# Two self-attention layers on one core: the rows of negated maxima by matmul and copy, or by two DMAs through device memory

## The chip, the cores and the metric

One core of a Trainium2 chip runs the whole program. The metric is device time in microseconds (us), the median of several executions; the profile comes from one further execution.

## What is computed

The input x has 4 images of 256 channels and 64 x 64 = 4096 positions. Layer 0 is self-attention over all positions, layer 1 is self-attention whose keys and values are max-pooled 2 x 2 to 1024 positions. Cut to what matters:

```
# layer 0, per image, xf = x as (256, 4096)
q = Wq @ xf + bq ; k = Wk @ xf + bk ; v = Wv @ xf + bv      # 32, 32, 256 rows
attn = softmax(q.T @ k, over the axis of q)
x = gamma * (v @ attn) + xf
# layer 1, on that x
theta = theta_w @ x + theta_b                               # 32 x 4096
phi, g = maxpool2(phi_w @ x + phi_b), maxpool2(g_w @ x + g_b)  # 32 x 1024, 128 x 1024
out = g @ softmax(theta.T @ phi, over the 1024).T
y = gamma * (out_w @ out + out_b) + x
```

All in float32. Softmax subtracts the row's maximum, so the maximum of each row of scores must be known before its exponentials.

## The kernel before

**Tiles, chunks and steps.** The 4096 columns that are softmaxed are cut into 8 chunks of 512 (`NCH`). A chunk of layer 0 takes 32 steps, one for each tile of 128 keys, a chunk of layer 1 takes 8. The order of images is layer 0, then layer 1, then the next image. In each step TensorE makes the scores of the tile that is `AHEAD` = 3 steps on (`scores`, L798), ScalarE takes two exponentials of them (L505 in float32, L508 rounded), GpSimd makes the rounding remainder `prob_l` (L446), VectorE adds the exponentials to a running sum `acc` (L637), and TensorE multiplies values by probabilities, three matmuls (L821, L824, L825) per half of the value rows: six in layer 0, three in layer 1 (`attend`).

**The maxima.** The scores are computed a first time, transposed, only for their maxima. A job `ST` is one matmul of 128 columns' queries against 512 keys into a PSUM bank (L861) and a VectorE `TENSOR_REDUCE` of it (L675, `maximum`). A chunk of layer 0 needs 32 of them, a chunk of layer 1 needs 8. They run one chunk ahead, between the other matmuls. After the last one VectorE reduces to four columns of negated maxima (L681), rounds them (L683) and takes the remainder (L684): pairs (high, low), one value per partition. They must become two rows of 512 columns under the queries, since the matmul of the scores adds them by two rows of ones in the keys. That is job `M`: TensorE transposes by four matmuls against the identity (L866), and VectorE copies the rows from PSUM to `queries` (L694). `scores` of a chunk's first tile waits for that copy (L793).

**Banks.** There are eight PSUM banks. X0 (`aux0`) and X1 (`aux1`) serve the jobs, Y is the second output bank where layer 1 doesn't use it. A job's matmul waits until the bank's last user has freed it: VectorE for `ST`, `D2`, `V0L`, ScalarE for `Z`.

**Other jobs.** `D1` and `D2` sum the exponentials and spread the reciprocals over partitions (L870, L698, L874); `Z` is the output projection of layer 1 (L878), copied out by ScalarE (L584) and added by GpSimd as `ZA` (L471); `N` is the residual add of layer 0 on GpSimd (L465); `X` and `XL` round the inputs (L546, L455); `K0`, `V0`, `K1`, `G1`, `T1` and their `..L` parts are projections (L835, L895) whose remainders VectorE makes (L653, L654).

**The order.** `make_plan` writes the order out by hand: `put(g, place, job)` hangs a job on step g; place 1 is before the first half of `attend`, place 2 between the halves, place 3 after. Each engine walks the same list and does its part of each job, in order. `before[...]` holds long lists at the start of layer 1. SyncE (queue SP) has its own loop: store a finished chunk (L415), wait for the store, load the chunk that is four on (L406).

Of the kernel before, what the change touches and what calls it, by code (L numbers as in the profile page):

```python
# [25 lines left out]
P = 128  # L26
DK = C // 8
# [65 lines left out]
def make_plan():  # L93
# [36 lines left out]
    for b in range(B):  # L130
        more = b + 1 < B
        for n in range(NCH):
            g = tile_no(0, b, n)
            prev = chunk_before(0, b, n)
            if prev is not None:
                put(g, 1, on(Job("D2", *prev, 0), X1))
                if prev[0] == 0:
                    c = prev[2]
                    put(g + 1, 1, Job("N", *prev, 0))
                    put(g + 3, 1, Job("N", *prev, 1))  # L140
                    put(g + 5, 1, Job("X", 1, b, c, 0))
                    put(g + 6, 1, Job("XL", 1, b, c, 0))
                    put(g + 8, 1, Job("XL", 1, b, c, 1))
                    put(g + 10, 1, on(Job("K1", 1, b, c, 0), X1))
                    put(g + 11, 1, Job("K1K", 1, b, c, 0), Job("K1Q", 1, b, c, 0))
                    put(g + 12, 1, Job("K1M", 1, b, c, 0), Job("K1L", 1, b, c, 0))
                    put(g + 13, 3, on(Job("G1", 1, b, c, 0), X1))
                    put(g + 15, 1, on(Job("T1", 1, b, c, 0), X1))
                    put(g + 16, 1, Job("T1L", 1, b, c, 0))
                else:  # L150
                    for k in range(CT):
                        put(g + 3 + 2 * k, 1, on(Job("Z", *prev, k), X1))
                        put(g + 4 + 2 * k, 1, Job("ZA", *prev, k))
            put(g + 22, 1, Job("XB", 0, b, n, 0))
            if n + 1 < NCH:
                steps = [(i, X0) for i in range(27)] + [(i, X1) for i in range(20, 25)]
                steps.sort()
                for i, (t, at) in enumerate(steps):
                    put(g + t, 1 if at == X1 else 3, maxima(0, b, n + 1, i // SUBS, i % SUBS, at))
                put(g + 28, 1, on(Job("M", 0, b, n + 1, 0), X1))  # L160
            else:
                for i in range(SUBS * (NCH - 1)):
                    put(g + i, 3, maxima(1, b, i // SUBS, 0, i % SUBS, X0))
# [28 lines left out]
        for n in range(NCH):  # L192
            g = tile_no(1, b, n)
            if n:
                prev = (1, b, n - 1)
                put(g, 1, on(Job("D2", *prev, 0), X0))
                for k in range(CT):
                    put(g + 2 + 2 * k, 3, on(Job("Z", *prev, k), X0))
                    put(g + 3 + 2 * k, 3, Job("ZA", *prev, k))
                if n + 1 < NCH:  # L200
                    put(g + 1, 1, on(Job("M", 1, b, n + 1, 0), Y))
# [3 lines left out]
            else:  # L205
                for s in range(SUBS):
                    put(g + s, 3, maxima(1, b, 1, 1, s, X0))
                put(g + 4, 3, on(Job("M", 1, b, 1, 0), X0))
            put(g + KT[1] - 1, 2, on(Job("D1", 1, b, n, 0), X0))
            if n + 2 < NCH:  # L210
                for s in range(SUBS):
                    put(g + 4 + s, 3, maxima(1, b, n + 2, 1, s, Y))
            if more:
# [3 lines left out]
                else:  # L217
# [747 lines left out]
```

## Time and profile before

| | us |
|---|---|
| three runs, median (lowest to highest) | 2790.31 (2786.36 to 2790.55) |
| the profiled execution, its own time | 2785.08 |
| its span, first to last instruction | 2783.3 |

Mean granted clock of TensorE: 0.984 of full speed. One chunk of layer 0 takes 64.3 us, one of layer 1 from 12.8 to some 22 us. The span has 39336 instructions. Times in the profile are from the span's start; L12 is line 12 of the kernel; "PE" is TensorE, "PEld" its weight loads, "DVE" VectorE, "ACT" ScalarE, "POOL" GpSimd, "SP" SyncE. Matmuls are pipelined: two matmuls of 512 columns start 0.23 us apart although each lasts 0.4 us, so a time on TensorE is read from start to start.

### The profile page before, as it was taken

The page shows a single profiled execution, that of the slowest core. Times are in us where ns is not written, and L with a number is a line of the kernel's source. Part 1 is how long each engine was busy: PE and PEld are TensorE (multiplying, and loading weights), DVE is VectorE, ACT ScalarE, POOL GpSimd, SP SyncE. Part 2 cuts the span into 40 slices and gives each one's busy share as a digit, 9 for nine tenths or more (in the row PEclk, how much of TensorE's full clock was granted, in tenths as well). Part 3 has the DMA queues.
Part 4 walks back from the last instruction along what each step waited for, and adds up shares of the span by engine and source line. Part 5 has one row for each costly group of instructions (what it writes and reads, how often), then busy time and mean ns, then how long its engine had stood idle before and what let it go on. Part 6 is the DMA issues. An engine that isn't in the chain of part 4 may idle for free.

```text
span 2783.3 us, 39336 instructions
## 1 busy us (share of the span) xinstructions
PE 2693.6 (97%) x12260; PEld 2159.1 (78%) x12260; DVE 2004.2 (72%) x3303; ACT 1745.2 (63%) x3171; POOL 1956.3 (70%) x1544
## 2 busy tenths in 40 slices
PE   7999999999999999998999999999899999999988
PEld 5788888877688888887778888888767888888866
DVE  7677777767767777776776777777676777777665
ACT  5566666666756666666765566666676666666657
POOL 3677777767767767776786767777577677777768
PEclk9999999999999999999999999999999999999989
DMA  2000000012110000001211000000121000000011
GB/s 86 1 16 24 16 24 16 16 39 69 61 38 16 24 16 16 16 16 38 69 65 35 24 16 16 16 16 16 46 76 61 16 16 16 16 16 16 16 46 61
DMA packets 43194, 85.03 MB, mean 31 GB/s; under 512 B 2672, under 2 KB 2800, under 8 KB 42992
## 3 DMA queue, kind: packets, MB, share of 16 engines
q1 hardware_dynamic: 35360, 68.17, 7.2%
q10 hardware_dynamic: 7632, 14.36, 1.8%
q8 instruction: 104, 1.70, 0.3%
q14 instruction: 98, 0.80, 0.1%
HBM read 48.96 MB, written 33.55 MB: 30 GB/s over the span
## 4 chain that ended last, share of the span: by engine, by line
PE 87%; DVE 4%; issue 3%; ACT 3%; POOL 2%; DMA 0%; POOLq 0%; ACTq 0%; DVEq 0%
PE o_ps L821 18%; PE o_ps L824 18%; PE o_ps L825 18%; PE s_ps L798 10%; PE aux L861 9%; PE aux L835 2%; PE aux L874 2%; PE aux L870 2%; DVE mx L675 2%; PE aux L895 1%; POOL prob_l L446 1%; PE aux L839 1%; PE aux L878 1%; ACT queries L530 1%; PE o_ps L861 1%
## 5 line engine op out<-in xcount | busy, mean ns | idle before, releaser
L446 POOL TENSOR_TENSOR prob_l<-prob,prob_h 128x512 fp32r<-128x512 f32 x1280 | 1640.6, 1289 | 717.4 <-ACT prob_h L508 706.0
L505 ACT ACTIVATE prob<-s_ps 128x512 f32<-128x512 f32 x1280 | 767.3, 599 | 819.8 <-PE s_ps L798 817.2
L675 DVE TENSOR_REDUCE mx<-aux 128x1 f32<-128x512 f32 x1103 | 760.7, 690 | 424.0 <-PE aux L861 419.0
L821 PE MATMUL o_ps<-prob_h,vh 128*128 128x512 f32 x2304 | 926.8, 402 | 0.5 <-ACT prob_h L508 0.4
L824 PE MATMUL o_ps<-prob_l,vh 128*128 128x512 f32 x2304 | 904.6, 393 | 1.4 <-POOL prob_l L446 1.3
L825 PE MATMUL o_ps<-prob_h,vl 128*128 128x512 f32 x2304 | 903.1, 392 | 0.0
L637 DVE TENSOR_TENSOR acc<-prob,acc 128x512 f32<-128x512 f32 x1216 | 836.4, 688 | 26.8 <-ACT prob L505 11.4
L508 ACT ACTIVATE prob_h<-s_ps 128x512 fp32r<-128x512 f32 x1280 | 762.1, 595 | 0.0
L798 PE MATMUL s_ps<-queries,keys 128*128 128x512 f32 x1280 | 524.3, 411 | 17.9 <-DVE queries L694 10.8
L824 PEld LDWEIGHTS o_ps<-prob_l,vh 128*128 128x128 f32 x2304 | 436.7, 190 | 97.7 <-POOL prob_l L446 5.0
L825 PEld LDWEIGHTS o_ps<-prob_h,vl 128*128 128x128 f32 x2304 | 434.6, 189 | 99.7
L821 PEld LDWEIGHTS o_ps<-prob_h,vh 128*128 128x128 f32 x2304 | 438.5, 190 | 94.4 <-ACT prob_h L508 3.4
L861 PE MATMUL aux<-keys,queries 96*128 96x512 f32 x1103 | 442.8, 401 | 14.2 <-ACT zc L584 5.1
L798 PEld LDWEIGHTS s_ps<-queries,keys 128*128 128x128 f32 x1280 | 245.7, 192 | 86.7 <-DVE queries L694 23.5
L861 PEld LDWEIGHTS aux<-keys,queries 96*128 96x128 f32 x1103 | 208.1, 189 | 77.0 <-DVE mx L675 15.9
L675 DVE TENSOR_REDUCE mx<-o_ps 128x1 f32<-128x512 f32 x159 | 109.2, 687 | 62.9 <-PE o_ps L861 62.3
L634 DVE COPY acc<-prob 128x512 f32<-128x512 f32 x64 | 44.3, 692 | 103.8 <-ACT psums L527 101.8
L455 POOL TENSOR_TENSOR xl<-xa,xh 128x512 fp32r<-128x512 f32 x72 | 92.1, 1285 | 24.9 <-ACT xh L546 24.9
L455 POOL TENSOR_TENSOR xl<-xp,xh 128x512 fp32r<-128x512 f32 x56 | 71.6, 1286 | 54.0 <-ACT xh L546 54.0
L465 POOL TENSOR_TENSOR xa<-osb,xa 128x512 f32<-128x512 f32 x64 | 83.2, 1303 | 20.9 <-DVE osb L707 20.9
L861 PE MATMUL o_ps<-keys,queries 96*128 96x512 f32 x159 | 83.6, 526 | 5.2 <-DVE mx L675 4.0
L471 POOL TENSOR_TENSOR xa<-zc,xa 128x512 f32<-128x512 f32 x64 | 83.1, 1300 | 6.0 <-ACT zc L584 4.8
(122 smaller groups left out, 1947.9 us busy)
## 6 DMA issues: line engine op xcount, KB each, us to landing
xa<-x SPq DMA_DIRECT2D x32, 512.0 KB, 3.7
spill<-xa SPq DMA_DIRECT2D x32, 512.0 KB, 2.7
xa<-spill SPq DMA_DIRECT2D x32, 512.0 KB, 3.7
y<-xa SPq DMA_DIRECT2D x32, 512.0 KB, 2.7
xp<-x ACTq DMA_DIRECT2D x26, 512.0 KB, 3.7
xp<-x SPq DMA_DIRECT2D x2, 512.0 KB, 9.1
prob<-w_in ACTq DMA_DIRECT2D x1, 576.0 KB, 5.3
wo<-w_out ACTq DMA_DIRECT2D x1, 128.0 KB, 6.1
```

The costliest lines, as they stand in the source:

```text
L446: nc.gpsimd.tensor_tensor(out=prob_l[:, i, :], in0=prob[:, i, :], in1=prob_h[:, i, :].bitcast(f32), op=ALU.subtract).then_inc(pl_ready, 1)
L455: nc.gpsimd.tensor_tensor(out=xl[r % 2][:, k, :], in0=src[:, k, :], in1=xh[r % 2][:, k, :].bitcast(f32), op=ALU.subtract).then_inc(xl_read ...
L465: nc.gpsimd.tensor_tensor(out=xa[slot][:, k, :], in0=osb[:, k, :], in1=xa[slot][:, k, :], op=ALU.add).then_inc(x1_ready, 1)
L505: nc.scalar.activation(prob[:, i, :], s_ps[s][:, :], ACT.Exp).then_inc(p_ready, 1)
L508: nc.scalar.activation(prob_h[:, i, :], s_ps[s][:, :], ACT.Exp).then_inc(ph_ready, 1)
L637: nc.vector.tensor_tensor(out=acc[:, :], in0=prob[:, i, :], in1=acc[:, :], op=ALU.add).then_inc(acc_done, 1)
L675: ins = nc.vector.tensor_reduce(out=dst, in_=bank[:, :], axis=AX.X, op=ALU.max)
L798: mm(s_ps[h % SRING][:, :], keys[l][:, t * P:(t + 1) * P], queries[:, q_slot(l, b, n), :], start=True, stop=True).then_inc(s_full, 1)
L821: mm(o_ps[ct][:, :], value(vh, l, t, ct), prob_h[:, i, :], start=t == 0, stop=False)
L824: mm(o_ps[ct][:, :], value(vh, l, t, ct), prob_l[:, i, :], start=False, stop=False)
L825: last = mm(o_ps[ct][:, :], value(vl, l, t, ct), prob_h[:, i, :], start=False, stop=t == KT[l] - 1)
L861: last = mm(dst[:, :], queries[0:R3, q_slot(l, b, c), sub * P:(sub + 1) * P], keys[l][0:R3, chunk(kc)], start=True, stop=True)
```

## The change

1. `M` leaves the banks, except for the very first chunk and the first chunk of layer 1 of each image (5 of 64). For the other 59, VectorE writes the pairs to a small tile `nm_pair`, SyncE stores it to device memory as two rows of 512 (`nm_rows`), waits for that store, and loads the two rows into `queries`. `scores` of the chunk's first tile waits for the second DMA (`nm_in`).
2. In layer 0 the 32 `ST` of a chunk end at step 23 and no longer at step 26; nine of them and no longer five are on X1, at place 1 of steps 1 to 4 and 19 to 23. `M` stands at step 25 in place of 28.
3. In layer 1 `M` stands at a chunk's step 0 in place of 1 (chunk 0: step 5, place 1, in place of step 4, place 3), and the last four `ST` of the next image's first chunk move from steps 0 and 1 of chunk 7 to steps 4 to 7 of chunk 6.
4. SyncE walks the same list as the other engines, so that its stores, loads and `M` stand in one order; the load behind a store of layer 1 is two steps later.
5. Score matmuls use 98 rows (96 and the pair) where they used 128.

The diff also has a second pair of names, `r_rows` and `scaled`, for `D2` by the same way; in this plan every `D2` is still in a bank, so nothing uses them.

```diff
             if n + 1 < NCH:
-                steps = [(i, X0) for i in range(27)] + [(i, X1) for i in range(20, 25)]
-                steps.sort()
-                for i, (t, at) in enumerate(steps):
-                    put(g + t, 1 if at == X1 else 3, maxima(0, b, n + 1, i // SUBS, i % SUBS, at))
-                put(g + 28, 1, on(Job("M", 0, b, n + 1, 0), X1))
+                steps = sorted(([(t, 3, X0) for t in range(23)]
+                         + [(t, 1, X1) for t in (1, 2, 3, 4, 19, 20, 21, 22, 23)]), key=lambda e: e[:2])
...
+                put(g + 25, 1, Job("M", 0, b, n + 1, 0))
...
                 if n + 1 < NCH:
-                    put(g + 1, 1, on(Job("M", 1, b, n + 1, 0), Y))
+                    put(g, 1, Job("M", 1, b, n + 1, 0))
...
-                put(g + 4, 3, on(Job("M", 1, b, 1, 0), X0))
+                put(g + 5, 1, Job("M", 1, b, 1, 0))
...
-                        put(g + s // 2, 3, maxima(0, b + 1, 0, n, s, (X1, Y)[s % 2]))
-                    put(g + 4, 1, on(Job("M", 0, b + 1, 0, 0), Y))
+                        put(g + 4 + s, 3, maxima(0, b + 1, 0, NCH - 1, s, Y))
+                if n == NCH - 1:
+                    put(g, 1, Job("M", 0, b + 1, 0, 0))
...
+                elif name == "M" and job in ROW_OF:
+                    i = ROW_OF[job]
+                    wait_free(sp, LAST_MAX[l, b, c])
+                    sp.dma_start(nm_rows[row].rearrange("h (s p) -> p (h s)", p=P),
+                                 nm_pair[:, :, :].bitcast(f32).rearrange("p h s -> p (h s)")).then_inc(nm_out, 16)
+                    sp.wait_ge(nm_out, 16 * (i + 1))
+                    wait(sp, nm_in, 16 * i)
+                    sp.dma_start(queries[NM, q_slot(l, b, c), :].bitcast(f32), nm_rows[row]).then_inc(nm_in, 16)
...
+                if rows in BANK:
+                    hi, lo = nm_wide[:, :, R3], nm_wide[:, :, R3 + 1]
+                else:
+                    hi, lo = nm_pair[:, 0, :], nm_pair[:, 1, :]
+                    wait(dve, nm_out, 16 * ROW_OF[rows])
+                chain(nc.vector.tensor_copy(hi, nm))
+                nc.vector.tensor_tensor(out=lo, in0=nm, in1=hi.bitcast(f32), op=ALU.subtract).then_inc(free[BANK[job]], 1)
...
                 if t == 0:
-                    wait_free(pe, Job("M", l, b, n, 0))
+                    rows = Job("M", l, b, n, 0)
+                    if rows in BANK:
+                        wait_free(pe, rows)
+                    else:
+                        pe.wait_ge(nm_in, 16 * (ROW_OF[rows] + 1))
...
-                mm(s_ps[h % SRING][:, :], keys[l][:, t * P:(t + 1) * P], queries[:, q_slot(l, b, n), :],
+                mm(s_ps[h % SRING][:, :], keys[l][0:R3 + 2, t * P:(t + 1) * P], queries[0:R3 + 2, q_slot(l, b, n), :],
                    start=True, stop=True).then_inc(s_full, 1)
```

**TensorE at steps 27 and 28 of a chunk of layer 0**, before (`s_ps` banks take the scores, `o_ps` the output, `aux1` is X1):

```order
L825 MATMUL o_ps1<-prob_h,vl0 128x512
L798 MATMUL s_ps1<-queries,keys0 128x512 [waits ph_ready]
L866 MATMUL aux1<-ident_r,nm_wide 128x128 [waits free0,free1]
L866 MATMUL aux1<-ident_r,nm_wide 128x128 x3
L821 MATMUL o_ps0<-prob_h,vh0 128x512 [waits ph_ready,free3]
```

In the change the four L866 rows are gone there, and on SP stand these (`free1` is the last maximum on X1):

```order
L455 DMA nm_rows<-nm_pair 128x8x1 [waits free1]
L459 DMA queries<-nm_rows 2x512 [waits nm_in,nm_out]
L433 DMA spill<-xa 128x2x512 [waits x1_ready]
L424 DMA xa<-spill 128x2x512 [waits xl_ready,xa_out0]
```

The rows' way moved from TensorE and VectorE to SP, ahead of the next chunk's store.

**TensorE at step 3 of chunk 0 of layer 0 of the second image**, before:

```order
L798 MATMUL s_ps2<-queries,keys0 128x512 [waits ph_ready]
L878 MATMUL aux1<-osb,wo 128x512 [waits free1]
L821 MATMUL o_ps0<-prob_h,vh0 128x512 [waits ph_ready,free3]
L824 MATMUL o_ps0<-prob_l,vh0 128x512 [waits pl_ready]
```

and now:

```order
L865 MATMUL s_ps2<-queries,keys0 128x512 [waits ph_ready]
L945 MATMUL aux1<-osb,wo 128x512 [waits free1]
L928 MATMUL aux1<-keys0,queries 128x512 [waits free5,free1]
L888 MATMUL o_ps0<-prob_h,vh0 128x512 [waits ph_ready,free3]
L891 MATMUL o_ps0<-prob_l,vh0 128x512 [waits pl_ready]
```

A matmul for maxima now follows `Z` (L945) into the same bank X1, ahead of the step's value matmuls. At step 19 of the same chunk one follows `V0` of step 17 in the same way, where X1 is freed by `V0L`, itself at step 19.

## Rows read from the trace of the kernel before

**Rows 1.** The page: busy time by engine, and the chain that ended last.

```profile
PE 2693.6 (97%) x12260; PEld 2159.1 (78%) x12260; DVE 2004.2 (72%) x3303; ACT 1745.2 (63%) x3171; POOL 1956.3 (70%) x1544
...
PE 87%; DVE 4%; issue 3%; ACT 3%; POOL 2%; DMA 0%; POOLq 0%; ACTq 0%; DVEq 0%
```

**Rows 2.** Windows: stretch, its length, busy us by engine, PEclk, DMA share, GB/s.

```profile
266.00:330.30 64.30, 64.30 (x290) 52.44 (x290) 47.24 (x78) 39.43 (x74) 45.98 (x36) 1.00 0.05 17
2695.10:2707.90 12.80, 12.71 (x62) 9.39 (x61) 9.69 (x19) 10.65 (x21) 12.55 (x11) 1.00 0.23 80
624.30:627.20 2.90, 2.90 (x14) 2.86 (x13) 1.14 (x2) 0.15 (x2) 2.73 (x3) 0.50 0.00 0
```

**Rows 3.** Timeline, TensorE, steps 28 and 29 of a layer-0 chunk: start, us, instruction.

```profile
321.79 0.56 PE L866 MATMUL aux<-ident_r,nm_wide 128*128 128x128 f32 x4
322.19 0.45 PE L821 MATMUL o_ps<-prob_h,vh 128*128 128x512 f32 x1
322.47 0.40 PE L824 MATMUL o_ps<-prob_l,vh 128*128 128x512 f32 x1
...
323.98 0.40 PE L821 MATMUL o_ps<-prob_h,vh 128*128 128x512 f32 x1
...
325.58 0.39 PE L821 MATMUL o_ps<-prob_h,vh 128*128 128x512 f32 x1
```

**Rows 4.** Waits: who waited for whom, us in total, times, longest.

```profile
PEld s_ps L798 <- DVE queries L694: 23.5, 39, 2.7
...
PE s_ps L798 <- DVE queries L694: 10.8, 8, 2.4
```

**Rows 5.** Timeline, chunk 0 of layer 1: the pairs ready, and the scores behind them.

```profile
619.01 0.17 DVE L684 TENSOR_TENSOR nm_wide<-aux,nm_wide 128x4 fp32r<-128x4 f32 x1
...
622.69 0.50 PE L798 MATMUL s_ps<-queries,keys 128*128 128x512 f32 x1 [2.36 <-DVE queries L694]
...
2676.16 0.17 DVE L684 TENSOR_TENSOR nm_wide<-aux,nm_wide 128x4 fp32r<-128x4 f32 x1
...
2677.89 0.50 PE L798 MATMUL s_ps<-queries,keys 128*128 128x512 f32 x1 [0.51 <-DVE queries L694]
```

**Rows 6.** Timeline, later chunks of layer 1: pairs ready, and scores at step 5.

```profile
727.00 0.17 DVE L684 TENSOR_TENSOR nm_wide<-o_ps,nm_wide 128x4 fp32r<-128x4 f32 x1
...
733.73 0.80 PE L798 MATMUL s_ps<-queries,keys 128*128 128x512 f32 x1
...
2709.61 0.17 DVE L684 TENSOR_TENSOR nm_wide<-o_ps,nm_wide 128x4 fp32r<-128x4 f32 x1
...
2716.51 0.40 PE L798 MATMUL s_ps<-queries,keys 128*128 128x512 f32 x1
```

**Rows 7.** Timeline, chunk 0 of layer 0, second image, steps 3 and 19.

```profile
761.70 1.02 PE L878 MATMUL aux<-osb,wo 128*128 128x512 f32 x2
...
762.87 0.79 ACT L584 ACTIVATE zc<-aux,cb,cols 128x512 f32<-128x512 f32 x1
...
798.38 0.40 PE L798 MATMUL s_ps<-queries,keys 128*128 128x512 f32 x1
...
799.79 0.68 DVE L653 TENSOR_TENSOR vl<-aux,vh 128x512 fp32r<-128x512 f32 x1
```

**Rows 8.** Timeline, steps 0 and 1 of a layer-0 chunk, then two reductions in layer 1.

```profile
330.85 1.40 DVE L707 SCALAR_TENSOR_TENSOR osb<-osb,cols,aux 128x512 f32<-128x512 f32 x2
...
332.19 0.40 PE L798 MATMUL s_ps<-queries,keys 128*128 128x512 f32 x1
...
704.49 1.28 DVE L675 TENSOR_REDUCE mx<-aux 128x1 f32<-128x512 f32 x2
```

**Rows 9.** DMA: a queue's packets and share, then issues, KB each, median us to landing.

```profile
q1 hardware_dynamic: 35360, 68.17, 7.2%
...
spill<-xa SPq DMA_DIRECT2D x32, 512.0 KB, 2.7
xa<-spill SPq DMA_DIRECT2D x32, 512.0 KB, 3.7
```

More of the change, by code:

```diff
@@ L272 @@
         LAST_READ.append(Job("G1", 1, _job.b, _job.c, 0) if _job.l else Job("V0", 0, _job.b, _job.c, 1))
+    if _job.name in ("M", "D2") and _job not in BANK:
+        ROW_OF[_job] = sum(j.name == _job.name for j in ROW_OF)
     if _job.name in ("K0", "V0", "K1Q", "K1K", "T1"):
@@ L429, in _, with entry @@
                     load_a(nxt // NCH % 2, nxt // (2 * NCH), nxt % NCH)
+            def entry(job):
+                name, l, b, c, k = job
+                row = chunk_no(l, b, c)
+                if name in ("N", "ZA") and k == CT - 1:
+                    store_a(l, b, c)
+                elif name == "XL" and l == 1 and k == CT - 1:
+                    reload(0, b, c)
+                elif name == "M" and job in ROW_OF:
[6 more added lines that the diff above has]
+                    sp.dma_start(queries[NM, q_slot(l, b, c), :].bitcast(f32), nm_rows[row]).then_inc(nm_in, 16)
+                elif name == "D1" and Job("D2", l, b, c, 0) in ROW_OF:
+                    i = ROW_OF[Job("D2", l, b, c, 0)]
+                    wait_free(sp, job)
+                    sp.dma_start(r_rows[row].rearrange("(s p) -> p s", p=P), rsum[:, :]).then_inc(r_out, 16)
+                    sp.wait_ge(r_out, 16 * (i + 1))
+                    wait(sp, scaled, i)
+                    sp.dma_start(rb[:, :], r_rows[row:row + 1, :].broadcast_to([P, CH])).then_inc(r_in, 16)
+            for p in range(ASLOTS + PSLOTS):
+                load_p(p)
+            late = {}
+            with nc.allow_non_contiguous_dma(reason="rows of one value per partition"):
+                for g in range(TILES):
+                    for job in late.get(g, ()):
+                        reload(*job[1:4])
+                    for job in BEFORE.get(g, ()):
+                        entry(job)
+                    for e in DURING.get(g, ()):
+                        entry(e.job)
+                        if e.job.name == "ZA" and e.job.k == CT - 1:
+                            late.setdefault(g + 2, []).append(e.job)
+                for job in END:
+                    entry(job)
             for slot in range(ASLOTS):
@@ L699, in entry @@
                 elif name == "D2":
-                    wait_full(dve, job)
+                    if job in BANK:
+                        wait_full(dve, job)
+                        recip, done = bank, free[BANK[job]]
+                    else:
+                        dve.wait_ge(r_in, 16 * (ROW_OF[job] + 1))
+                        recip, done = bank, scaled
                     dve.wait_ge(o_act, chunk_no(l, b, c) + 1)
@@ L865, in entry @@
                     for s in range(SUBS):
[L866 removed]
+                        last = mm(dst[0:R3 + 2, s * P:(s + 1) * P], nm_wide[:, s, :], ident_r[:, :], start=True, stop=True)
                 elif name == "D1":
```

91 lines of the change are left out of this document (49 added, 42 removed).

## The prediction

> **What bounds the kernel now.** I read the page first: TensorE is busy 97% of the span and holds 87% of the chain that ended last [rows 1]. The windows say where this is literally so. A chunk of layer 0 is 64.30 us with TensorE busy for all of them, VectorE for 47.24, GpSimd for 45.98 [rows 2]: in layer 0 a matmul that goes is time that goes, and a wait of TensorE that comes is time that comes. In layer 1 it is narrower: a chunk of the last image takes 12.80 us with GpSimd busy for 12.55 [rows 2], so TensorE can give back 0.25 us there before GpSimd takes over. The remaining question is how job `M` sits in this, and that is read from the timeline and the waits.
>
> **What the removed job costs.** At step 28 the four transposes start at 321.79, and the second value matmul at 322.47 [rows 3]. Five single steps apart from it, value matmuls are 1.60/7 = 0.229 us apart (323.98 to 325.58 is one step of seven matmuls [rows 3]), so without `M` that second matmul would stand at 321.79 + 0.23: `M` costs 0.45 us of TensorE. From 322.47 to 323.98 are six matmuls, which is 1.37 us at that pace; it took 1.51. The 0.14 us are the scores waiting for VectorE's copy of the rows, part of the 23.5 us in 39 times that weight loads of the scores wait for L694 [rows 4]. So a chunk of layer 0 gives back 0.45 + 0.14 = 0.59 us, and 28 of them **16.5 us**. In layer 1, chunks 1 to 6 carry one `M` each: for three images 18 x 0.45 = **8.1 us**, for the last one GpSimd caps it, 6 x 0.25 = **1.5 us**. `M` of the next image's first chunk (3) stands in chunk 7, where steps have four matmuls and GpSimd is the longer: nothing. VectorE's copies (59) are at nothing too, since VectorE has 17 us to spare per layer-0 chunk [rows 2]; its part in the critical stretches of layer 1 is inside the 0.45 us. Score matmuls with 98 rows in place of 128: matmuls of 96 rows already run at the same pace beside them, so nothing. Sum of gains: 26.1 us.
>
> **What the two DMAs take.** No row shows such a DMA, 1024 runs of 4 bytes out and two rows of 2 KB back, so I bound it. A 512 KB store lands 2.7 us after issue; queue 1 spent 7.2% of 16 x 2783.3 us on 35360 packets, 0.091 us each [rows 9]. The store's 256 packets on 16 DMA engines are then 16 x 0.091 = 1.5 us, and 1.2 us are fixed. The load, 3.7 us, has 2.2 us fixed on the same reckoning [rows 9]. First hop: 64 packets per engine. At no cost for their few bytes it takes 1.2 us, at a full packet's 0.091 us each 7.0. Second hop: one packet on each of a few engines, 1.2 to 3.7 us. Together 2.4 to 10.7 us. I take **4.5 us**, nearer the lower end: 4 KB in total are less than a hundredth of the store's bytes, and the row it is nearest to in bytes is the fixed part of store and load, 1.2 + 2.2 = 3.4 us, to which I add 1.1 for the 64 small packets. The Trainium skill, DMA: Bandwidth & Descriptors, section Anatomy of one DMA, gives about 2 us fixed to any DMA of GpSimd's queue, whatever its size; two such in place of the 3.4 us would make the sum 2.4 us higher (0.6 us at four waits). The trace's store, on SyncE's queue, is below it with 1.2.
>
> **Where the scores would wait.** The window is from the pairs being ready to the scores of the next chunk. Layer 1, the narrowest of the first image: 727.17 to 733.73, less the 0.45 us of `M` that was in it, 6.1 us; last image 2709.78 to 2716.51, 6.3 us [rows 6]. Layer 0: the last maximum is now at step 23 and the scores at step 29, a step with one extra matmul (1.83 us) and five of 1.60, 9.8 us, less some 2.9 us (an estimate: two reductions and a sum at 0.64 each, and the matmul and the small operations around them) until the pairs are ready: 6.9 us. 4.5 us fit in all of them. They don't fit in chunk 0 of layer 1, where the maxima of chunk 1 end at step 3 and the scores stand at step 5: pairs ready at 619.18, scores at 622.69 after a wait of 2.36 already [rows 5]. With 4.5 us they go to 623.7, 1.0 us later, three times; in the last image 2676.33 + 4.5 = 2680.8 against 2677.89, 2.9 us later [rows 5]. Sum **5.9 us**. Behind these waiting scores on TensorE stands everything else of it, and ScalarE, GpSimd and VectorE run dry after it. On SP nothing urgent is queued behind an `M`; but `M` is queued behind a load of 512 KB in the chunks of layer 1, which can add up to its 2.2 us to the first hop, inside the window at 4.5.
>
> **What the packing costs.** Per chunk of layer 0 the same 32 matmuls and reductions remain. Steps 1 to 4 now have two. At step 1 the one on X1 needs `D2` off the bank: VectorE ends at 330.85 + 1.40 = 332.25, TensorE would come at 332.19 + 0.23 = 332.42 [rows 8]: no wait, by 0.15 us. In a step with two, TensorE needs 9 x 0.23 = 2.07 us and VectorE three operations of 0.64 (two reductions in a row take 1.28 [rows 8]), 1.92 us: it keeps up. So nothing in the ordinary chunk. In chunk 0 of the next image (three times) X1 has other users. At step 3 the matmul follows `Z` at once: it could start at 761.70 + 0.46 = 762.16 and must wait for ScalarE's copy, done at 763.66 [rows 7]: 1.5 us. At step 19 it could start at 798.38 + 0.23 and must wait for `V0L`, done at 800.47 [rows 7]: 1.85 us. 3 x 3.35 = **10.1 us**. Moving four `ST` from chunk 7 to chunk 6 of layer 1 adds 4 x 0.23 = 0.9 us there and takes as much off chunk 7, in which TensorE is left with little and GpSimd, 12.55 us in a chunk [rows 2], is the longer: I count even.
>
> **The clock.** After the wait of 2.36 us the granted clock was 0.50 from 624.30 to 627.20 [rows 2], the 1.2 GHz level instead of 2.4: half of 2.9 us, 1.5 us lost. How short a wait may be and still be followed by one I can't read from this. Of the six new waits and the longer one in the last image I let half be followed by one: 3.5 x 1.5 = **5.3 us**.
>
> **Sum:** -26.1 + 5.9 + 10.1 + 5.3 = -4.8 us. The profiled execution took 2785.1 us, so 2780.3 for its like; the median shown is 2790.3, so **2785.5 us**, 0.17% less. A measurement of this kernel tells about 0.2% (5.6 us) from no change.
>
> **Rivals.** *1. As summed* (0.42): between about -10 and +3 us, as the clock and the second digit of the hops fall; mostly within 0.2%, 0.12 of it beyond on the fast side, 0.02 on the slow. *2. The new waits on X1 are cheaper* (0.24): if ScalarE and VectorE stand earlier than in the rows, or what TensorE loses comes back since its neighbours catch up, 10.1 + 5.3 us shrink to some 3, and the sum is -17: 2773 us. For it: ScalarE idles before L584's step; against: in layer 0 TensorE has no slack in which it could catch up [rows 2]. *3. Long hops* (0.20), the other side: it decides where the two DMAs exceed the windows, from 6.1 us on. At 7 us, chunk 1 costs 10 us more than summed, layer 1 about 9 for some 12 narrow chunks at 0.7 to 0.9, layer 0 3 us: +17, 2807 us; every further microsecond costs some 50 us. Upper bounds of both hops give 10.7 us, so the rows don't exclude it. For a mechanism: each 4-byte run is its own packet, and the packets may cost far more than their bytes. The Trainium skill, same page, Specifications, says a transfer under 512 B becomes a read-modify-write, which is this rival; no packet like it is in this trace. *4. The packed steps bind* (0.07): the 0.15 us at step 1 is missing and each chunk loses 0.4 us more, 11 us: +6, 2797 us. *5. The rows' way was hidden anyway* (0.07), so that the change doesn't give what it says: another engine holds each place, layer 0's 16.5 us are half, +3 us: 2794 us.
>
> **How the numbers follow.** Faster: 0.12 + 0.24 = 0.36. Within 0.2%: 0.28 + 0.04 of rival 4 + 0.06 of rival 5 = 0.38. Slower: 0.02 + 0.20 + 0.03 + 0.01 = 0.26. The likeliest is case 1, alone 2779 to 2793. The range reaches to rival 2 and to rival 3 at 7 us, 2772 to 2807, and leaves out longer hops.
>
> **What would show it.** Right: the value matmuls of layer 0 run through at 0.23 us with no gap where L866 was; L866 has 20 matmuls; the DMA part lists `nm_rows<-nm_pair` and `queries<-nm_rows` at some 2.7 and 1.8 us, 59 each; the waits list scores for a DMA four times, 3.4 us for the first three and about 3.5 for the last; L928 waits three times each for L584's successor and for `V0L`. Wrong: scores waiting for a DMA 28 times in layer 0 or throughout layer 1 (hops over 6 us), waits of VectorE's reductions in steps 1 to 4, or L928 without those six waits.

## The result, and the profile after

| | us |
|---|---|
| before, four runs, median (lowest to highest) | 2788.8 (2786.4 to 2790.6) |
| the change, four runs | 3203.5 (3200.1 to 3207.3) |
| ratio, 95% interval | 1.149 (1.147 to 1.151) |
| the profiled execution of the change, its span | 3198.3 |

The change makes the kernel 415 us slower. The page of its profile: busy time by engine, then the chain that ended last, by engine and by line (cf. [rows 1]):

```profile
PE 2792.8 (87%) x12024; PEld 2216.5 (69%) x12024; DVE 1961.2 (61%) x3244; ACT 1748.2 (55%) x3171; POOL 1955.7 (61%) x1544
...
PE 66%; DMA 24%; DVE 6%; issue 2%; ACT 1%; POOL 0%; POOLq 0%; ACTq 0%; DVEq 0%
```

A quarter of the chain is now DMA, where it was 0%. The waits for it (engine, what for: us in total, times, longest; cf. [rows 4]):

```profile
PEld s_ps L865 <- DMA queries<-nm_rows: 357.5, 59, 13.2
...
PE s_ps L865 <- DMA queries<-nm_rows: 328.8, 59, 12.8
...
PE aux L928 <- DVE vl L706: 5.2, 3, 1.7
```

All 59 rows that come by DMA are waited for, 5.6 us each on average, where I expected four waits. One of them in the chain of waits (start, us, what), at the end of the first chunk of layer 0:

```profile
124.31 0.17 DVE nm_pair L743
124.48 0.02 issue
124.50 9.38 DMA nm_rows<-nm_pair
133.87 0.02 issue
133.89 3.24 DMA queries<-nm_rows
137.13 0.04 issue
137.17 0.80 PE s_ps L865
```

The pairs are ready at 124.48, the scores start 12.7 us later after a wait of 5.34. Without it they would have stood at 131.8: the window is 7.3 us (I had worked out 6.9), and the hops are what does not fit. The store alone takes 9.38. The view of the DMA engines for 124.4 to 134.0, in 40 slices of 0.24 us, shows where:

```profile
DMA  0000576000000000000000000000000000000000
...
DMA packets 1040, 0.00 MB, mean 0 GB/s; under 512 B 1040, under 2 KB 1040, under 8 KB 1040
```

All packets lie in three slices, some 0.9 to 1.6 us after the issue. Then the engines do nothing that a row shows, for nearly 8 us, until the store counts as done. Over the whole run the DMA part says the same (KB each, median us to landing; cf. [rows 9]):

```profile
nm_rows<-nm_pair SPq DMA_DIRECT2D x59, 4.0 KB, 10.6
```

The clock adds to it. Windows at the same wait (columns as in [rows 2]):

```profile
133.00:137.20 4.20, 0.03 (x1) 0.03 (x1) 0.00 (x0) 0.00 (x0) 0.00 (x0) 0.64 0.01 1
137.20:141.00 3.80, 3.80 (x9) 3.04 (x10) 0.00 (x0) 1.09 (x3) 1.27 (x1) 0.50 0.00 0
141.00:145.00 4.00, 4.00 (x22) 3.42 (x22) 1.57 (x3) 2.65 (x5) 2.43 (x2) 1.00 0.00 0
```

TensorE idles, and for 3.8 us after it the granted clock is 0.50, the 1.2 GHz level: half of 3.8 us, 1.9 us, is lost behind the wait. The mean granted clock fell from 0.984 to 0.925. At half speed in the slow stretches that is 2 x 0.075 x 3198 = 480 us of them, 391 us more than before. By the clock's records in the trace 155 us of them lie inside the 59 waits, where they cost nothing. The other 236 us cost half of their length, 118 us or 2.0 us for each wait.

A chunk of layer 0, from one reciprocal to the next (287.57 to 359.49), takes 71.9 us where it took 64.3 [rows 2].

### The profile page after: what moved, and what is told of

It reads as the page before. It is cut to its first block, busy times and chain, and to the rows that moved or that the text cites. A ratio compares the mean times of both kernels' runs of the same rounds, so it can differ in the third digit from the quotient of the medians.

```text
span 3198.3 us, 38986 instructions
## 1 busy us (share of the span) xinstructions
PE 2792.8 (87%) x12024; PEld 2216.5 (69%) x12024; DVE 1961.2 (61%) x3244; ACT 1748.2 (55%) x3171; POOL 1955.7 (61%) x1544
## 4 chain that ended last, share of the span: by engine, by line
PE 66%; DMA 24%; DVE 6%; issue 2%; ACT 1%; POOL 0%; POOLq 0%; ACTq 0%; DVEq 0%
DMA nm_rows<-nm_pair 19%; PE o_ps L888 14%; PE o_ps L891 14%; PE o_ps L892 14%; PE s_ps L865 8%; PE aux L928 8%; DMA queries<-nm_rows 4%; DVE mx L728 2%; PE aux L902 2%; DVE acc L690 1%; PE aux L941 1%; PE aux L937 1%; PE aux L906 1%; PE aux L962 1%; PE o_ps L928 1%
## 5 line engine op out<-in xcount | busy, mean ns | idle before, releaser
L888 PE MATMUL o_ps<-prob_h,vh 128*128 128x512 f32 x2304 | 956.8, 415 | 0.5 <-ACT prob_h L561 0.4
L891 PE MATMUL o_ps<-prob_l,vh 128*128 128x512 f32 x2304 | 939.5, 408 | 1.3 <-POOL prob_l L499 1.3
L892 PE MATMUL o_ps<-prob_h,vl 128*128 128x512 f32 x2304 | 929.0, 403 | 0.0
L865 PE MATMUL s_ps<-queries,keys 98*128 98x512 f32 x1280 | 554.6, 434 | 338.7 <-DMA queries<-nm_rows 328.8
L865 PEld LDWEIGHTS s_ps<-queries,keys 98*128 98x128 f32 x1280 | 260.0, 204 | 425.1 <-DMA queries<-nm_rows 357.5
L891 PEld LDWEIGHTS o_ps<-prob_l,vh 128*128 128x128 f32 x2304 | 456.6, 198 | 108.0 <-POOL prob_l L499 3.1
L888 PEld LDWEIGHTS o_ps<-prob_h,vh 128*128 128x128 f32 x2304 | 459.1, 199 | 100.5 <-issue 2.7
L892 PEld LDWEIGHTS o_ps<-prob_h,vl 128*128 128x128 f32 x2304 | 453.2, 197 | 108.8
L928 PE MATMUL aux<-keys,queries 96*128 96x512 f32 x1097 | 449.7, 410 | 15.5 <-DVE vl L706 5.2
L508 POOL TENSOR_TENSOR xl<-xp,xh 128x512 fp32r<-128x512 f32 x56 | 71.5, 1285 | 71.7 <-ACT xh L599 69.1
L928 PE MATMUL o_ps<-keys,queries 96*128 96x512 f32 x165 | 93.2, 565 | 7.5 <-DVE mx L728 6.3
## 6 DMA issues: line engine op xcount, KB each, us to landing
nm_rows<-nm_pair SPq DMA_DIRECT2D x59, 4.0 KB, 10.6
```

The costliest lines, as they stand in the source:

```text
L508: nc.gpsimd.tensor_tensor(out=xl[r % 2][:, k, :], in0=src[:, k, :], in1=xh[r % 2][:, k, :].bitcast(f32), op=ALU.subtract).then_inc(xl_read ...
L865: mm(s_ps[h % SRING][:, :], keys[l][0:R3 + 2, t * P:(t + 1) * P], queries[0:R3 + 2, q_slot(l, b, n), :], start=True, stop=True).then_inc(s ...
L888: mm(o_ps[ct][:, :], value(vh, l, t, ct), prob_h[:, i, :], start=t == 0, stop=False)
L891: mm(o_ps[ct][:, :], value(vh, l, t, ct), prob_l[:, i, :], start=False, stop=False)
L892: last = mm(o_ps[ct][:, :], value(vl, l, t, ct), prob_h[:, i, :], start=False, stop=t == KT[l] - 1)
L928: last = mm(dst[:, :], queries[0:R3, q_slot(l, b, c), sub * P:(sub + 1) * P], keys[l][0:R3, chunk(kc)], start=True, stop=True)
```

## The experiments

A run of bytes, in "runs of 4 B", is a stretch of neighbouring bytes in what the DMA writes. "By matmul" is job `M` as before the change; "packed" is point 2 of the change, "unpacked" the steps before it. Medians against the kernel before, timed beside them (2788.3 to 2789.6):

| kernel | rows of maxima by | else | us | ratio (95%) |
|---|---|---|---|---|
| the change | two hops, runs of 4 B | packed, 98 rows | 3203.5 | 1.149 (1.147 to 1.151) |
| E1 | matmul | packed, 98 rows | 2802.7 | 1.004 (1.003 to 1.006) |
| E2 | hops in layer 0 alone | packed, 98 rows | 2989.7 | 1.072 (1.070 to 1.073) |
| E3 | two hops, 4 B | unpacked, 98 rows | 3287.0 | 1.178 (1.176 to 1.180) |
| E4 | two hops, 16 B | packed, 98 rows | 2812.3 | 1.008 (1.006 to 1.009) |
| E5 | one hop, 16 B | packed, 98 rows | 2802.1 | 1.004 (1.003 to 1.005) |
| E6 | one hop, 16 B | E5 without clashes | 2792.6 | 1.001 (1.000 to 1.002) |
| E7 | matmul, every fourth column | packed, 98 rows | 2827.2 | 1.014 (1.012 to 1.015) |
| E8 | VectorE | unpacked, 98 rows | 2866.4 | 1.028 (1.026 to 1.029) |
| E9 | two hops, 128 B | E6's packing, 98 rows | 2782.2 | 0.997 (0.996 to 0.999) |
| E10 | matmul | unpacked, 98 rows | 2799.3 | 1.004 (1.002 to 1.005) |
| E11 | matmul | unpacked, 128 rows | 2787.5 | 0.999 (0.998 to 1.000) |
| E12 | two hops, 128 B | E6's packing, 128 rows | 2765.6 | 0.992 (0.990 to 0.994) |
| **E13** | E12, chunk 1 of layer 1 by matmul | 128 rows | **2756.4** | **0.989 (0.987 to 0.990)** |
| E14, E15, E16 | the kernel before | 98, 127, 112 rows | 2804.3, 2801.2, 2805.5 | 1.006, 1.005, 1.006 (each +-0.002) |

### Where the 415 us are: E1, E2, E3

E1 takes the rows' DMAs out of the change and leaves the rest.

```diff
-                put(g + 25, 1, Job("M", 0, b, n + 1, 0))
+                put(g + 28, 1, on(Job("M", 0, b, n + 1, 0), X1))
```

(and the three other `M` of layer 1 and the next image likewise, as before the change; E2 does it for those three alone, so 28 rows of layer 0 are left with hops.)

> The change with its packing, SyncE's order and 98 rows, but all rows of maxima made by TensorE and VectorE as before (step 28 in layer 0). Theory (all of the loss is the hops): within 2790 to 2805 us, likeliest 2797, the six waits on X1 in chunk 0 of images 1 to 3 and nothing else. Rival (the packed steps bind, or SyncE's order delays transfers): a good part of the 415 us stays, 2850 us or more.

> The change with the two hops in the 28 ordinary chunks of layer 0 only; the 31 others made by matmul and copy. Theory (each row pays its own wait of 5.3 us and some 1.6 us of halved clock, less 0.59 us gained): 28 x 6.3 = 176 us over the kernel with all rows by matmul, about 2970 us (2950 to 2995). Rival (the waits in layer 0 feed on those of layer 1, for instance by the clock): under 2930 us, or the loss nearly whole, over 3050.

E1 took 2802.7, E2 2989.7. So the parts of the change add up: 14 us without any hop, 187 us for the 28 rows of layer 0 (6.7 each), 214 us for the other 31 (6.9 each). Per row, on average over the change: a wait of 5.6 us, some 2.0 of clock behind it, less what `M` gave. Nearly all of the loss is the hops.

E3 keeps the hops and spreads layer 0's maxima over steps 0 to 26 again (27 on X0, five on X1, the lines that the diff removed).

> The change's hops in both layers, but layer 0's maxima spread over steps 0 to 26 as before. Theory (the wait is the hops' 12.7 us less the window between the pairs and the scores): the window shrinks by about 6 us in 28 chunks, 170 us more than the change: about 3370 us (3310 to 3410). Rival (the packing buys nothing, since the transfers are held by something later): within 30 us of 3204.

It took 3287.0, 84 us more than the change, under my range. A chunk of layer 0 went from 71.7 to 76.6 us, so the packing buys 4.9 us of window there and not 6; the chunks of layer 1, summed over four images, took 37 us less than in the change, which I can't explain (the store's median was 9.7 us there, not 10.6). What it shows: given such hops, packing was worth its place.

### What a store of 4-byte runs costs: DMAs alone

Both kernels leave all of the computation out: SyncE issues a DMA, waits for it, issues the next, six of each kind. The 4-byte store is the change's own, and the others differ as the expectation says.

```diff
+                for i in range(REPS):
+                    step(sp.dma_start(d_rows[i].rearrange("h (s p) -> p (h s)", p=P),
+                                      pair[:, :, :].rearrange("p h s -> p (h s)")))
...
+                for i in range(REPS):
+                    step(sp.dma_start(d_apart[i][:, :, 0], pair[:, :, :].rearrange("p h s -> p (h s)")))
```

> Nothing of the layers is computed: SyncE alone issues small DMAs one after the other, each waited for before the next, six of each kind, then copies x to y; its total time means nothing here. Issue to landing of the first hop's store (1024 runs of 4 B into device memory) was 10.6 us in the changed kernel, the load 3.2 us to the scores. Theory A (the number of single 4 B writes to device memory sets it): 1024 runs about 10 us, 512 runs about 6, 256 runs about 4, 256 runs of 16 B about 4, 128 runs of 32 B about 3, 1024 runs of 4 B that lie 64 B apart as slow as those side by side, about 10. Theory B (writes that fall on the same memory line wait for each other): the 1024 runs 64 B apart take under 5 us, those side by side 10. Theory C (load by the kernel's own transfers and engines): all of them take 2 to 3 us here. The load of 2 rows of 2 KB: 2 us in all. The single hop from SBUF to SBUF, 128 runs of 16 B into one row: 2 to 2.5 us by A and B.

The timeline of SyncE's queue (start of the first of six, us to the end of the last issue): one DMA takes a sixth of the time from one group's start to the next group's.

```profile
1.48 48.74 SPq L338 DMA_DIRECT2D rows4b<-pair  x6
60.37 43.25 SPq L341 DMA_DIRECT2D half4b<-pair  x6
113.65 38.70 SPq L343 DMA_DIRECT2D quarter4b<-pair  x6
159.70 7.36 SPq L345 DMA_DIRECT2D pairs32b<-pair  x6
168.14 18.13 SPq L347 DMA_DIRECT2D apart4b<-pair  x6
189.00 6.27 SPq L349 DMA_DIRECT2D two2kb<-flat  x6
196.25 6.95 SPq L351 DMA_DIRECT2D queries<-rows4b  x6
204.43 32.59 SPq L353 DMA_DIRECT2D gathered<-pairs32b  x6
241.91 9.39 SPq L356 DMA_DIRECT2D runs16b<-pair  x6
252.49 9.99 SPq L358 DMA_DIRECT2D onehop<-pair  x6
263.88 17.02 SPq L360 DMA_DIRECT2D onehop<-wide  x6
283.67 0.48 SPq L362 DMA_DIRECT2D onehop<-pair  x1
```

1024 runs of 4 B: (60.37 - 1.48) / 6 = 9.8 us, with nothing else running, so theory C falls. 512 of them 8.9, 256 of them 7.7: the number of runs is not it either, and theory A falls. The same 1024 runs 64 B apart, a partition's eight behind each other: 3.5 us. 128 runs of 32 B 1.4, 256 runs of 16 B 1.8, two rows of 2 KB 1.2, the load of two rows 1.4. A load that gathers 1024 runs of 4 B takes 6.2, so turning the order round on the way back would be no remedy. One hop from SBUF to SBUF takes 1.9 in 128 runs of 16 B and 3.3 in 512 runs of 4 B, where 512 such runs took 8.9 into device memory, so 4 B runs are not so dear where they end in SBUF.

The second kernel varies the distance alone, with neighbouring runs from neighbouring partitions.

> Small DMAs alone again, none of the layers computed: a store of 1024 runs of 4 B from 128 partitions into device memory, the same every time but for the distance of the runs there: 4, 8, 16, 32, 64 B (16, 8, 4, 2 and 1 writes to a line of 64 B, an assumed size). In the first look they took 9.8 us at 4 B and 3.5 us at 64 B. Theory (writes into one line wait for each other, about 0.4 us each): 9.8, 6.7, 5.0, 4.2 and 3.5 us. Rival (a line of 32 B or less, or the span of addresses matters): 3.5 us from 32 B on alike, or 9.8 us at 8 B too. The last kind, eight runs of 4 B of one partition side by side: by the theory 8 writes to 32 B, 16 to a line, about 9.8 us; if only writes from different partitions disturb each other, 4 us or less.

```profile
0.93 48.00 SPq L328 DMA_DIRECT2D every4b<-pair  x6
59.47 21.84 SPq L331 DMA_DIRECT2D every8b<-pair  x6
85.67 14.83 SPq L334 DMA_DIRECT2D every16b<-pair  x6
103.32 14.25 SPq L337 DMA_DIRECT2D every32b<-pair  x6
120.02 12.66 SPq L340 DMA_DIRECT2D every64b<-pair  x6
134.70 36.91 SPq L343 DMA_DIRECT2D own32b<-wide  x6
179.71 0.42 SPq L346 DMA_DIRECT2D big<-x  x1
```

By distance: 9.8 us at 4 B, 4.4 at 8, 2.9 at 16, 2.8 at 32, 2.4 at 64 (3.5 in the first kernel, whose 64 B runs lay in another order). It is steepest at the close end, not 0.4 us per write as my theory had it, and it flattens from 16 B on. Eight runs of one partition side by side, with the next partition's eight behind them, take 7.5, so it isn't writes of different partitions alone. What is shown: neighbouring 4 B writes to device memory delay each other's completion, by 7 us in this shape. The size of the line on which they meet isn't: a fixed 64 B line fits the last steps badly.

The Trainium skill, DMA: Bandwidth & Descriptors, Anatomy of one DMA, says of GpSimd's path that most of a DMA's fixed cost is the memory's receipt for the last byte, without which the semaphore can't rise. The nearly 8 idle us after the last packet look like it, on SyncE's queue. The whole fixed cost is about 2 us by the Trainium skill; here the wait behind the last packet alone is nearly four times as much.

### Mending the store: E4, E5, E9

E4 changes which column belongs to which maximum: partition p holds columns 4p to 4p + 3, so its four values are 16 B in a row.

```diff
-                    last = mm(dst[:, :], queries[0:R3, q_slot(l, b, c), sub * P:(sub + 1) * P],
+                    cut = queries[0:R3, q_slot(l, b, c), sub * P:(sub + 1) * P]
+                    if Job("M", l, b, c, 0) not in BANK:
+                        cut = queries[0:R3, q_slot(l, b, c), :].rearrange("r (p s) -> r s p", s=SUBS)[:, sub, :]
+                    last = mm(dst[:, :], cut,
...
-                    sp.dma_start(nm_rows[row].rearrange("h (s p) -> p (h s)", p=P),
+                    sp.dma_start(nm_rows[row].rearrange("h (p s) -> p h s", p=P),
```

> The change with one thing different: the four maxima of a partition belong to four neighbouring columns (the queries of a maximum's matmul are every fourth column), so the first hop writes 256 runs of 16 B and no longer 1024 of 4 B. Alone such a store took 1.8 us and the load 1.4. Theory (the form of the store is the whole loss): hops of 5 to 6 us in the kernel, inside the windows except in chunk 1 of layer 1; the kernel with all rows by matmul took 2802.7, less the 26 us that the rows' way gives, plus some 8 in chunk 1: 2785 us (2772 to 2805). Rival (the kernel's own traffic makes any first hop long, or the two hops never fit): over 2900 us.

2812.3 us, 391 us less than the change, by the form of one 4 KB store. It now lands after 2.1 us, and four or five waits are left, in chunk 1 of layer 1:

```profile
nm_rows<-nm_pair SPq DMA_DIRECT2D x59, 4.0 KB, 2.1
```

The prediction's 2.7 us for the first hop would have been near for this store. But 2812 is 27 us over what I expected. E5 keeps these columns and drops device memory: two DMAs, one a row, go from `nm_pair` straight to `queries`.

> As the last, but without device memory: two DMAs, one a row, go from the pairs straight to the queries' rows; alone both together took 2.5 us. Theory: no wait for rows anywhere or under 1 us in chunk 1 of layer 1: 2802.7 - 26 = 2777 us (2765 to 2790). Rival (matmuls whose weights are every fourth column are slower, or other costs of the rows' way): as much above that as L928 has grown, some 0.05 us x 1056 = 50 us.

2802.1 us: the second hop was worth 10 us, but again 25 us are missing. The rival's own row had grown. Weight loads of the maxima's matmuls, in E1 and then in E5 (busy us, mean ns):

```profile
L928 PEld LDWEIGHTS aux<-keys,queries 96*128 96x128 f32 x1097 | 207.8, 189 | 95.4 <-DVE mx L728 15.9 <-ACT zc L637 12.0 <-DVE vl L706 6.6
```

```profile
L930 PEld LDWEIGHTS aux<-keys,queries 96*128 96x128 f32 x1097 | 335.2, 306 | 86.9 <-DVE mx L727 13.3 <-ACT zc L636 11.7 <-DVE vl L705 6.5
```

0.31 us is longer than the 0.23 from one matmul to the next. E7 adds only that to E1, with VectorE's copy putting the rows in order:

> The kernel with all rows by matmul (2802.7 us) with one thing added: the maxima's matmuls take every fourth column of the queries as weights, and VectorE's copy puts the rows back in order. The one-hop kernel took as long as the kernel with all rows by matmul, though it lacks 236 transposing matmuls; its weight loads of that kind took 0.31 us where they took 0.19. Theory (these loads outlast a matmul's 0.23 us and give back what the rows' way gains): some 0.02 us x 1262 more, about 2824 us (2814 to 2835). Rival (the gain of 26 us was never there, TensorE's transposes were hidden): within 4 us of 2803.

2827.2, 24.5 us over E1, 0.019 us for each of 1262 loads. So E4 and E5 had the gain and gave it back in strided weights.

E9 keeps columns in natural order. VectorE transposes the pairs in 32 x 32 blocks first (0.21 us), the store is 128 runs of 128 B, the load 32 of 128 B.

```diff
+                    chain(pair)
+                    nc.vector.transpose(nm_turned[:, :].bitcast(f32), nm_pair[:, :, :].bitcast(f32).rearrange("p h s -> p (h s)")).then_inc(
+                        free[BANK[job]], 1)
...
+                    sp.dma_start(nm_rows[row], nm_turned[:, :].bitcast(f32)).then_inc(nm_out, 16)
...
+                    sp.dma_start(queries[NM, q_slot(l, b, c), :].bitcast(f32).rearrange("h (s q j) -> h s q j", s=SUBS, q=SUBS),
+                                 nm_rows[row].rearrange("(q x h s) j -> x h s q j", x=4, h=2, s=SUBS)[0]).then_inc(nm_in, 16)
```

> Two hops through device memory as in the change, columns in their natural order, but VectorE first transposes the pairs in blocks of 32 x 32, so that the store is 128 runs of 128 B and the load 32 runs of 128 B; packing without the clashes on X1. Theory (form of the store and of the weights both mended): hops of 4 to 5 us fit, except in chunk 1 of layer 1; the one-hop kernel without clashes took 2792.6, less 20 for the weights, plus up to 10 for the second hop: 2780 us (2770 to 2793). Rival (through device memory it stays long): over 2850 us.

2782.2 us. Four times the bytes of the change's store, and it lands in 1.4 us; the waits that are left are four, 11.8 us, for chunk 1 of layer 1 (waits, then the DMA part):

```profile
PE s_ps L875 <- DMA queries<-nm_rows: 11.8, 4, 3.9
```

```profile
nm_rows<-nm_turned SPq DMA_DIRECT2D x59, 16.0 KB, 1.4
```

### The clashes, the packing and the rows: E6, E10, E11, E14 to E16

E6 is E5 with no maximum on X1 at steps 3, 4 and 19 of chunk 0 of images 1 to 3.

```diff
+                if b and not n:
+                    steps = [(t, 3, X0) for t in range(25)] + [(t, 1, X1) for t in (1, 2, 20, 21, 22, 23, 24)]
```

> The last kernel with the two clashes on X1 taken away: in chunk 0 of images 1 to 3 no maximum on X1 at steps 3, 4 and 19, two more at place 3 of steps 23 and 24 and one on X1 at 24. Theory (the matmul kernel's 14 us over before are these clashes, with the halved clock after them): 10 us under the last kernel, 2767 us (2755 to 2780). Rival (the 14 us are spread over all packed steps): within 3 us of the last kernel.

9.4 us less than E5 (2792.6): the clashes, foreseen at 10.1, measured. The figure itself missed 2767 by the 25 us that E5 had missed.

E10 is E1 with the maxima unpacked (E3's steps).

> All rows by matmul, layer 0's maxima spread over steps 0 to 26 as before; left of the change are SyncE's order, 98 rows, and the four maxima moved to chunk 6 of layer 1. Theory (the packing alone costs the 14 us of the matmul kernel: 11 in the three turns between images, 0.25 us in each ordinary chunk of layer 0): 2789 us (2784 to 2794). Rival (SyncE's order or the moved maxima cost part of it): 2796 us or more.

2799.3, a miss: 10 us stay that I had put down to the packing. Chunks of layer 0 are longer without packing (64.8 us) than with (64.5 in E1): in an ordinary chunk packing gives 0.3 us, 8 us in all, and that hid most of the clashes' 9.4 us from this comparison. Left in E10 were SyncE's order, the four moved maxima and 98 rows. E11 puts 128 rows back; E14 is the kernel before with 98 rows, and E15 and E16 the same with 127 and 112:

```diff
-                mm(s_ps[h % SRING][:, :], keys[l][:, t * P:(t + 1) * P], queries[:, q_slot(l, b, n), :],
+                mm(s_ps[h % SRING][:, :], keys[l][0:R3 + 2, t * P:(t + 1) * P], queries[0:R3 + 2, q_slot(l, b, n), :],
```

> The last kernel with all rows by matmul and nothing packed (2799.3 us) with one thing put back: the scores' matmuls read 128 rows of keys and queries again (rows 98 to 127 of the queries are zero) and not 98. In that kernel a chunk of layer 0 took 64.85 us where it took 64.25 before, and from one value matmul to the next were 0.2343 us in place of 0.2316. Theory (98 rows are what makes layer 0 slower, by 0.6 us in each of 28 chunks): 2785 us (2778 to 2792). Rival (SyncE's order does it, or the difference is chance): 2796 us or more.

> The kernel before with one thing changed: its scores' matmuls read 98 rows of keys and queries and not 128. Theory (98 rows make layer 0 slower): 2803 us (2796 to 2808). Rival (they change nothing): within 3 us of 2789; then SyncE's order is what remains.

> The kernel before with 127 rows in its scores' matmuls. With 98 rows it took 2804.3 us, with 128 it takes 2788.7. Theory (any switch between matmuls of all 128 rows and of fewer costs the same; the scores' matmul stands between a value matmul of 128 rows and a maximum's of 96): about 2804 us (2798 to 2809). Rival (the price goes with the rows left out): under 2793 us.

> The same with 112 rows. Theory (any number under 128 costs the same): 2804 us (2798 to 2809). Rival (the price goes with the rows left out, 0.5 us a row): 2796 us (2793 to 2799).

E11 2787.5 and E14 2804.3: 98 rows cost 12 us taken out of the one and 15.6 us put into the other, and SyncE's order and the moved maxima nothing that can be seen. The 14 us of E1 are then 9.4 for the clashes and 12 to 16 for 98 rows, less the packing's 8. With 127 rows it is 12.9, with 112 it is 17.2: the price comes with the first row that is left out, and by these runs (each known to some 5 us) it does not grow with the rows. The rows of E14 that show it, two scores' matmuls a step of eight apart, and then two of E11:

```profile
211.11 0.40 PE L798 MATMUL s_ps<-queries,keys 98*128 98x512 f32 x1
...
212.96 0.40 PE L798 MATMUL s_ps<-queries,keys 98*128 98x512 f32 x1
```

```profile
209.97 0.40 PE L866 MATMUL s_ps<-queries,keys 128*128 128x512 f32 x1
...
211.81 0.40 PE L866 MATMUL s_ps<-queries,keys 128*128 128x512 f32 x1
```

1.85 against 1.84 us: in one step it drowns in the rounding. Averaged over the 432 steps of this form in six chunks of layer 0 of each image it is 1.864 us in E14 (and in E15) against 1.844 in E11. Most of it lies between value matmuls that follow each other, 234.5 ns from start to start against 231.6, though these read 128 rows in both kernels; so the price doesn't sit at the switch between matmuls of different rows, as E15's expectation had it. From reciprocal to reciprocal E14 takes 64.8 us (267.03 to 331.88), E11 64.3 (270.97 to 335.25); 28 x 0.55 = 15 us, which is the price. Why the value matmuls run 1% slower isn't shown. The Trainium skill, TensorE: Matmul & The Clock Gate, LDWEIGHTS, says that a weight load takes the same time whatever the number of rows; the mean load of these matmuls, 192 to 193 ns in either form, agrees, but the stream around it does not stay the same.

### Without TensorE and without DMA: E8

VectorE transposes `nm_wide` in blocks and copies four pieces of 2 x 128 into `queries`; unpacked.

```diff
+                    chain(nc.vector.transpose(nm_turned[:, :, :], nm_wide[:, :, R3:P].bitcast(f32)))
+                    rows = queries[NM, q_slot(l, b, c), :].rearrange("r (s q j) -> r q s j", s=SUBS, q=SUBS)
+                    for q in range(SUBS):
+                        last = nc.vector.tensor_copy(rows[:, q], nm_turned[32 * q:32 * q + 2, :, :])
```

> The rows leave TensorE without any DMA: VectorE transposes the pairs in blocks of 32 x 32 and copies the four pieces into the queries' rows; layer 0's maxima end at step 26 as before, columns in their natural order, and the next image's first maxima stand in chunk 7 as before. Theory (what the prediction counted as gain, 26 us, is there as soon as nothing waits for a hop and no step is packed): 2789 - 26 = 2763 us (2755 to 2775). Rival (another engine holds each of these places, or VectorE's five small operations cost what its one copy did not): 2783 us or more.

2866.4, a miss by 100 us. VectorE's timeline at a row, and the scores behind it:

```profile
129.07 0.30 DVE L744 STREAM_TRANSPOSE nm_turned<-nm_wide 128x128 f32<-128x128 f32 x1
129.41 2.27 DVE L747 CAST queries<-nm_turned 2x128 fp32r<-2x128 f32 x4
```

```profile
131.73 0.50 PE L860 MATMUL s_ps<-queries,keys 98*128 98x512 f32 x1 [1.26 <-DVE queries L747]
```

Each piece of 128 elements takes 0.57 us, where the one copy of 512 elements it replaces took 0.70. With the transpose that is 2.6 us on VectorE in place of 0.7, TensorE waits 61 us for it in all, and sums and maxima come later. So it doesn't tell whether the gain of 26 us exists; E9, E12 and E13 bear on it.

### The version that beats both: E12, E13

E12 is E9 with 128 rows. E13 also makes the rows of chunk 1 of layer 1 by matmul, as before.

```diff
-                put(g + 5, 1, Job("M", 1, b, 1, 0))
+                put(g + 4, 3, on(Job("M", 1, b, 1, 0), X0))
```

> The kernel with two hops in blocks (2782.2 us) with 128 rows in the scores' matmuls. Theory (98 rows cost it what they cost the others): 10 to 15 us less, 2770 us (2762 to 2777). Rival: within 4 us of 2782.

> The last kernel with the rows of chunk 1 of layer 1 made by matmul as before, since the two hops came 2.9 us late there four times (11.8 us of waits in the kernel with blocks). Theory (these waits are paid in full, less a matmul's row and VectorE's copy): 8 us under the last kernel, 2762 us (2754 to 2770). Rival (ScalarE or VectorE holds chunk 1 anyway): within 3 us of it.

2765.6 and 2756.4 us. E13 is 1.1% faster than the kernel before, and its page reads like [rows 1] again:

```profile
PE 2658.2 (96%) x12040; PEld 2133.4 (77%) x12040; DVE 1973.1 (72%) x3304; ACT 1744.0 (63%) x3171; POOL 1954.2 (71%) x1545
```

TensorE has 35 us less to do than before, and its chunk of layer 0 takes 63.6 us (268.78 to 332.37) where E11's takes 64.3.

## Why the prediction was wrong

I forecast 2785.5 us (2772 to 2807); it took 3203.5.

- **What bounds the kernel**: right. TensorE fills layer 0, and each microsecond that it waits is paid.
- **The removed job, 26.1 us**: right as a sum, but part of it belongs to the packing, which I had at nothing. E13 is 31 us under E11, which differs from it in the rows' way and the packing. In layer 0 a chunk gave 0.7 us where I had 0.59, and the eight chunk lengths of layer 1, summed over four images, 13.1 us (636.4 to 623.3) where I had 9.6. With 98 rows the two can be told apart: a chunk of layer 0 takes 64.8 us with `M` unpacked (E10), 64.5 with `M` packed (E1), 64.1 with hops that fit, packed (E9). E1 less its clashes (2802.7 - 9.4) against E9 less its four waits (2782.2 - 9.2, by E13) leaves 20 us for the job alone, an estimate. For 128 rows no run tells them apart.
- **What the two DMAs take, 4.5 us**: this step failed. They take 12.7 (9.4 and 3.2). The second hop lies inside its bounds of 1.2 to 3.7. The first was bounded by 7.0 us, from the cost of a full packet times 64 packets an engine, and the chosen value went down from there because 4 KB is little. But a packet of 4 B costs next to nothing (1040 of them in 0.7 us); the time is in the completion of neighbouring writes. No row of before shows a store of that form, so the upper bound was no bound: it priced each packet as if only its passage through the engine could cost. The trace of before does hold one transfer in runs far below 512 B, against what the prediction says: `cols<-columns`, 4.5 KB in 128 runs of 36 B, 6.5 us from issue to landing. It is a load, at the kernel's start behind two larger ones, so it prices no store, but it did say that few bytes need not mean a short DMA.
- **The windows**: right (6.9 against 7.3 us in layer 0), and with them the deciding point of rival 3, hops over 6.1 us. Of the four, that rival is the one that came true. Its own reason, that small packets may cost far more than their bytes, is not it, since they were through in 0.7 us. The read-modify-write under 512 B, which the prediction puts beside it from the Trainium skill (DMA: Bandwidth & Descriptors, Specifications), is nearer to what the runs show, but none shows one, and 4 B writes 64 B apart, as far under 512 B, took 2.4 to 3.5 us. The rival's price was too low: by "some 50 us for every further microsecond" hops of 12.7 us would give 2807 + 5.7 x 50 = 3092, 112 us short, which is about what the clock behind the waits comes to, 59 x 2.0 us. It had a fifth of the chances, and the range stopped at 7 us, inside my own bounds of 2.4 to 10.7.
- **Chunk 1 of layer 1, 5.9 us**: right in kind. With hops that fit, the four waits of E9 are these and no others, and taking them away gave 9.2 us.
- **The packing, 10.1 us**: right, within 2 us. E6 gives 9.4 for both clashes; in the change the one with `V0L` is there three times, 1.74 us each against 1.85, and the one with `Z` three times, 0.98 us each against 1.5. That ordinary chunks pay nothing is right too; they gain 0.3 us.
- **The clock**: I let half of the waits be followed by 1.5 us. In the trace 57 of the 59 have a stretch at 0.50 within 8 us behind them, and the loss comes to 2.0 us for each wait.
- **98 rows, nothing**: wrong, 15.6 us. I argued that matmuls of 96 rows run at the same pace beside them. They do, but once the scores' matmuls use fewer rows as well, the value matmuls beside them slow by 1%, which only means over many steps or a whole chunk's length show.

That last step and the first hop were my two costs of "nothing" or "little" for a form that no row showed.

## What to carry to other kernels

Before moving a column of single values through device memory, look at the length of its runs there: turn the data first (a transpose of 128 x 32 values in blocks of 32 x 32 took 0.21 us) so that a partition or a block writes 16 B or more in a row, and the pairs land in 1.4 us (128 B) to 2.1 us (16 B) and not 10. Where the longer runs are bought with weights at a stride, as in E4, look at the weight loads as well. A DMA's price is its issue to its landing, not its packets' time, and where none of its form is in the trace, time it alone before it is put behind a window of 7 us. What an edit does "beside" the main idea, here 98 rows for 128, needs its own run.

## What I had not expected of the hardware

- 1024 stores of 4 B took 9.8 us side by side in device memory and 2.4 or 3.5 us, by their order, when 64 B apart, though in the kernel the packets were through within 1.6 us of issue; 256 of them side by side still took 7.7.
- Scores' matmuls of 127, 112 or 98 rows in place of 128 cost the kernel 12.9, 17.2 and 15.6 us, most of it between value matmuls that themselves kept 128 rows.
- A weight load from every fourth column took 306 ns and one from neighbouring columns 189, and 1262 of them cost 24.5 us.
- A VectorE copy of 2 x 128 elements into two partitions took 0.57 us, one of 2 x 512, in E10, 0.70. Which of its features costs (the rounding, the pieces of 32, the shift across partitions) wasn't tried.
